# A vision-transformer tower: attention 1's projection and the gates in 16-bit halves, GpSimd adding exponentials and making low halves, and another order of the steps

## The reference

```python
h = layernorm(layernorm(patches) @ W + b)          # 196 x 768 -> 196 x 192, class row put before
x = layernorm(h)
q, k, v = split(x @ w_qkv.T)                        # 12 heads of 64
q, k = q * rsqrt(norm_over_heads(q) + eps), k * rsqrt(norm_over_heads(k) + eps)
h = h + softmax(q k^T / scale) v @ w_out.T + b_out  # attention 1, projection 768 -> 192
x = layernorm(h)
probs = softmax(x @ Wg.T + bg)                      # 8 experts, top 2 kept
delta = low_rank(x, A, ba, Bm, bb, combine)         # rank 16 for each expert
qkv = x @ Wqkv.T + bqkv + delta                     # attention 2, 12 heads of 16
h = h + softmax(q k^T * 0.25) v @ Wproj.T + bproj
```

## Time and profile before

| | |
|---|---|
| median of 3 runs | 3112.13 us (3110.72 to 3112.16) |
| the profiled execution's own time | 3109.35 us |
| its span | 3107.6 us |
| mean granted TensorE clock | 0.988 |
| busy shares of the span | PE 95%, PEld 78%, DVE 75%, ACT 63%, POOL 19% |

### The profile page before, as it was taken

How to read it: one execution, slowest core, us unless ns; L and a number is a source line. 1 busy time by engine, 2 the same in 40 slices (tenths; PEclk the granted TensorE clock), 3 DMA queues, 4 the chain that set the end, 5 groups by cost and what they waited for, 6 DMA issues and landing times.

```text
span 3107.6 us, 98361 instructions
## 1 busy us (share of the span) xinstructions
PE 2962.8 (95%) x41624; PEld 2428.5 (78%) x41624; DVE 2329.0 (75%) x5441; ACT 1963.4 (63%) x3777; POOL 594.1 (19%) x859
## 2 busy tenths in 40 slices
PE   5899999999999999999999999999999999999996
PEld 4788878877877877877877877888788778778775
DVE  5777777777777777777777777777777777777773
ACT  2566666666666666666666666666666666666663
POOL 3112112111111121121121121121121111111210
PEclk7999999999999999999999999999999999999998
DMA  4000000000000000000000000000000000000000
GB/s 116 9 22 22 12 22 16 17 22 12 21 22 12 21 22 12 22 22 12 22 22 12 22 22 12 22 22 12 22 15 18 22 12 21 22 12 22 14 4 7
DMA packets 28389, 61.28 MB, mean 20 GB/s; under 512 B 4210, under 2 KB 18389, under 8 KB 27958
## 3 DMA queue, kind: packets, MB, share of 16 engines
q1 hardware_dynamic: 27958, 54.98, 6.1%
HBM read 45.29 MB, written 9.68 MB: 18 GB/s over the span
## 4 chain that ended last, share of the span: by engine, by line
PE 59%; DVE 35%; ACT 3%; issue 3%; POOL 0%; DMA 0%; SPq 0%; DVEq 0%; ACTq 0%
PE psum L686 9%; DVE mx L1119 8%; PE psum L695 8%; PE psum L590 8%; PE psum L612 7%; PE psum L674 4%; PE psum L722 4%; PE psum L622 4%; DVE st L1008 3%; PE psum L656 3%; DVE mx L1132 2%; PE psum L725 2%; DVE qk L1211 2%; PE psum L732 2%; PE psum L617 2%
## 5 line engine op out<-in xcount | busy, mean ns | idle before, releaser
L850 ACT ACTIVATE ebufs<-psum 99x788 f32<-99x788 f32 x768 | 592.0, 823 | 57.9 <-PE psum L674 45.2
L519 POOL TENSOR_TENSOR veps<-mv,eps_ln 99x2 f32<-99x2 f32 x256 | 116.7, 456 | 2266.5 <-DVE mv L1041 1344.9
L1132 DVE TENSOR_REDUCE mx<-psum 99x4 f32<-99x788 f32 x384 | 357.5, 974 | 137.5 <-PE psum L639 137.2
L1119 DVE TENSOR_REDUCE mx<-psum 99x4 f32<-99x788 f32 x384 | 362.9, 974 | 52.1 <-PE psum L631 52.1
L612 PE MATMUL psum<-hn_s,qk_w 128*128 128x197 f16 x3840 | 354.1, 249 | 14.9 <-DVE hn_s L1083 7.4
L612 PEld LDWEIGHTS psum<-hn_s,qk_w 128*128 128x128 f16 x3840 | 322.2, 97 | 35.6 <-DVE qk L1211 19.0
L686 PE MATMUL psum<-ebufs,vx 98*32 98x197 f32 (+1 forms) x6144 | 293.7, 330 | 0.0
L590 PE MATMUL psum<-emb_w,xb 128*99 128x193 f32 x1536 | 264.0, 327 | 0.0
L695 PE MATMUL psum<-out_w,qk 128*99 128x192 f32 x1536 | 263.8, 328 | 0.1
L590 PEld LDWEIGHTS psum<-emb_w,xb 128*99 128x99 f32 x1536 | 249.1, 166 | 1.4 <-issue 0.9
L686 PEld LDWEIGHTS psum<-ebufs,vx 98*32 98x32 f32 (+1 forms) x6144 | 201.4, 110 | 57.2
(11 more groups left out here) (172 smaller groups left out, 6442.7 us busy)
## 6 DMA issues: line engine op xcount, KB each, us to landing
xb<-x_t SPq DMA_DIRECT2D x64, 591.0 KB, 3.8
out<-h SPq DMA_DIRECT2D x128, 73.5 KB
out<-h SPq DMA_DIRECT2D x64, 0.8 KB
vx<-w_qk SPq DMA_DIRECT2D x2, 384.0 KB, 7.8
qk_sq<-w_emb SPq DMA_DIRECT2D x1, 576.0 KB
vx<-w_qk SPq DMA_DIRECT2D x1, 576.0 KB, 5.6
out_w<-w_out SPq DMA_DIRECT2D x8, 72.0 KB
late<-w_lora_b SPq DMA_DIRECT2D x1, 480.0 KB
```

Source lines behind the costliest of these rows:

```text
L850: nc.scalar.activation(ebuf[n].rearrange("p e a t -> p e (a t)"), psum[0:TR, b + 2 * half:b + 2 * half + 2, 0:2 * NT], ACT.Exp).then_inc(r ...
L1119: nc.vector.tensor_reduce(mx[s][:, :, 2 * i:2 * i + 2].rearrange("p a e -> p e a"), psum[0:TR, b:b + 2, 0:2 * NT].rearrange("p e (a t) -> ...
L1132: nc.vector.tensor_reduce(mx2[s][:, :, at:at + 2].rearrange("p a e -> p e a"), psum[0:TR, b + 2 * half:b + 2 * half + 2, 0:2 * NT].rearran ...
```

## The change

1. **Projection of attention 1 (`OP`).** `out_w` is held in two fp16 halves (split at the start, scaled by 64), and the attention output in `o_h` and `o_l`. ACT copies `o_t` to `o_h` (a new instruction of step `M`), POOL subtracts for `o_l` (a new step `ML.0` to `ML.2`), and PE runs three fp16 matmuls in place of one fp32 matmul: 36 for an image. `OP` waits for `o_low` of `ML.2`.
2. **Gates (`G`).** The weights are split too, and PE takes the fp16 halves of the hidden rows that exist already: 10 fp16 matmuls in place of 4 fp32. ACT's fp32 copy in `T2` is gone.
3. **Sums of exponentials (`PV`).** POOL adds the two key tiles of each `ST` step into `esum` (three buffers), and PE sums 4 matmuls for each `PV` instead of 8; they now stand between the two halves of the product with v. So that the 98-row tile may be added to the 99-row one, row 99 of tile 0 is driven to zero through `head_sel0` and a constant of -30000.
4. **Maxima (`NT`, `NT2`).** The tables `neg` are fp16, and the transposes are fp16 matmuls with an fp16 identity.
5. **Patches.** One buffer `xb` in place of two; the load of the next image is issued after the `EMB` step has read it.
6. **Order.** Another table `ORDER`.

```diff
-+X T1@4 =QK2.0@1 =QK2.1@0 QK.0@2 =SM2.0@4 QK.1@0 QK.2@2 =SM2.1@4 -ST.3@0 -ST.4@4 -ST.5@2 -PV.1@6 S
+QK.0@0 -NT@7 =G@3 =GB QK.1@4 -ST.0@0 -ST.1@2 -ST.2@6 =T3@4 QK.2@0 S -ST.3@6 =QK2.0@2 =QK2.1@5
...
-        xb = two("xb", [128, KC, NT])
+        xb = sb("xb", [128, KC, NT])
...
+        ESUMS = 3
+        esum = [sb(f"esum{i}", [TR, 2, NT]) for i in range(ESUMS)]
...
+                    elif p[0] == "ML":
+                        i = p[2]
+                        wait(pool, now, o_high, ("M", s, i))
+                        nc.gpsimd.tensor_tensor(o_l[s][:, 2 * i:2 * i + 2, :], o_t[s][:, 2 * i:2 * i + 2, :],
+                                                o_h[s][:, 2 * i:2 * i + 2, :], ALU.subtract).then_inc(o_low[1], 1)
+                    elif p[0] == "ST":
+                        wait(pool, now, rd_sig["ST"], p)
+                        n = st_order.index(p) % ESUMS
+                        wait_free(pool, now, esum_users[n], sums_used)
+                        e = exp_tile(p)
+                        nc.gpsimd.tensor_tensor(esum[n][:], e[:, :, 0, :], e[:, :, 1, :], ALU.add
+                                                ).then_inc(tiles_added[1], 1)
...
-                        mm = transposes(p, lambda t, n: table[0:n, t], 128)
+                        for t in range(2):
+                            n = key_rows(t)
+                            mm = nc.tensor.matmul(ps(p, slice(0, 128), slice(TO * t, TO * t + n)),
+                                                  table[0:n, t], ident_h[0:n, 0:n], start=True, stop=True)
...
-                        for c in (2, 0, 1):
+                        for c in (0, 2, 1):
+                            if c == 2:
+                                wait(pe, now, tiles_added, ("ST", s, 2 * i + 1))
+                                for j in range(4):
+                                    es = esum[st_order.index(("ST", s, 2 * i + j // 2)) % ESUMS]
+                                    mm = nc.tensor.matmul(ps(p, slice(32 * j, 32 * j + 32), slice(0, NT), 1),
+                                                          ones_col[:], es[:, j % 2, :], start=True, stop=True)
+                                mm.then_inc(sums_made[1], 1)
+                                continue
...
-                        wait(pe, now, rd_sig["PV"], ("M", s, 2))
+                        wait(pe, now, o_low, ("ML", s, 2))
                         for t in range(2):
                             for m in range(H // 2):
-                                mm = nc.tensor.matmul(ps(p, slice(0, TR), slice(D * t, D * t + D)),
-                                                      o_t[s][:, m, tile_cols(t)], out_w[:, m, :],
-                                                      start=(m == 0), stop=(m == H // 2 - 1))
+                                for n, (left, w) in enumerate(((o_h, 0), (o_h, 1), (o_l, 0))):
+                                    mm = nc.tensor.matmul(ps(p, slice(0, TR), slice(D * t, D * t + D)),
+                                                          left[s][:, m, tile_cols(t)], out_w[:, w, m, :],
+                                                          start=(m + n == 0), stop=(m == H // 2 - 1 and n == 2))
...
-                            for c in range(2):
+                            for n, (w, v, c) in enumerate(PACKED):
                                 mm = nc.tensor.matmul(ps(p, slice(0, TR), slice(136 * t, 136 * t + 136)),
-                                                      hn2_t[s][:, c, tile_cols(t)], gl_w[:, c, :],
-                                                      start=(c == 0), stop=(c == 1))
+                                                      hn2_s[s][:, v, c, tile_cols(t)], gl_w[:, w, :],
+                                                      start=(n == 0), stop=(n == 4))
...
-                        if kind == "T2":
-                            nc.scalar.copy(hn2_t[s], src)
...
+                    elif kind == "M":
+                        wait(act, now, rd_sig["PV"], p)
+                        nc.scalar.copy(o_h[s][:, 2 * i:2 * i + 2, :], o_t[s][:, 2 * i:2 * i + 2, :]).then_inc(o_high[1], 1)
```

More of the change, by code:

```diff
@@ L51 @@
 ORDER = """
-+X T1@4 =QK2.0@1 =QK2.1@0 QK.0@2 =SM2.0@4 QK.1@0 QK.2@2 =SM2.1@4 -ST.3@0 -ST.4@4 -ST.5@2 -PV.1@6 S
--M.1 =SM2.2@0 -PV.2@4 PS@1 =NT2@7 -M.2 N.0 N.1 N.2 +EMB@2 -OP@3 N.3 =ST2.0@4 V.0@0 SM.0@2 =ST2.1@4
--LD =V2@0 SM.1@4 SM.2@2 -T2@6 =PV2.0@7 SM.3@4 =M2.0 =ST2.2@0 =PV2.1@6 SM.4@4 SM.5@0 -G@7 =PV2.2@2
-NT@4 V.1@0 ST.0@4 =M2.1 ST.1@6 +LA =M2.2 -GB +LB ST.2@2 =OP2@5 -T3@4 +LC PV.0@6 M.0
+QK.0@0 -NT@7 =G@3 =GB QK.1@4 -ST.0@0 -ST.1@2 -ST.2@6 =T3@4 QK.2@0 S -ST.3@6 =QK2.0@2 =QK2.1@5
+-PV.0@6 -M.0 -ML.0 =SM2.0@0 PS@4 =V2@6 N.0 -ST.4@0 -PV.1@4 -ST.5@6 -M.1 =SM2.1@0 -ML.1 +X =SM2.2@4
+N.1 -PV.2@0 -M.2 -ML.2 N.2 +EMB@5 =NT2@0 +LA N.3 =ST2.0@0 -OP@6 SM.0@2 SM.1@0 =ST2.1@4 -LD =PV2.0@4
+SM.2@6 =ST2.2@0 =M2.0 =PV2.1@5 +LB V.0@6 =M2.1 -T2@2 =PV2.2@4 +LC SM.3@6 =M2.2 V.1@0 +T1@5 SM.4@2
+SM.5@6 =OP2@4
 """
@@ L243, in vit_tower @@
         o_t = [qk[s][:, 0:H // 2, :] for s in range(2)]
+        o_h = [qk[s][:, 6:9, :].rearrange("p m t -> p (m t)").bitcast(F16).rearrange("p (m t) -> p m t", m=6) for s in range(2)]
+        o_l = [qk[s][:, 9:12, :].rearrange("p m t -> p (m t)").bitcast(F16).rearrange("p (m t) -> p m t", m=6) for s in range(2)]
         gl = two("gl", [TR, 2, NE + NE * RANK])
@@ L353, in reader, with release @@
             return rd_sig[p[0]], ({"PV": "M", "PV2": "M2"}.get(p[0], p[0]), *p[1:])
+        def release(q, freed, earlier):
+            sig, r = freed
+            assert earlier or POS[r] >= POS[q]
+            return sig, r, earlier and POS[r] >= POS[q]
         def wait_free(eng, now, order, freed):
             q, earlier = now.previous(order, now.at)
-            wait(eng, now, *freed(q), earlier)
+            wait(eng, now, *release(q, freed(q), earlier))
         def passes(eng, body):
@@ L401, in vit_tower, with sums_used @@
             bias_loads.append((low_row[r], mats[low:low + NE + 1, 259:261]))
+        st_order = steps["made_ST"]
+        esum_users = [st_order[n::ESUMS] for n in range(ESUMS)]
+        def sums_used(p):
+            return sums_made, ("PV", p[1], p[2] // 2)
         def squares_used(p):
@@ L434, in body @@
                 for kind, s, i in now.steps():
-                    if kind == "QK" and i == 0 and now.which in ("first", "middle"):
+                    if kind == "EMB":
                         wait(sp, now, pe_sig["EMB"], ("EMB", s, 0))
-                        wait(sp, now, xsq_ready, ("X", s, 0))
-                        load(now.it + 1, s)
+                        n = now.image((kind, s, i)) + s
+                        if n < ITERS:
+                            load(n, 1 - s)
                     elif kind == "OP2":
@@ L785, in body @@
                                 act.wait_ge(setup_dve, 2)
-                        nc.scalar.activation(xsq_first if first else xsq, xb[s][:], ACT.Square
+                        nc.scalar.activation(xsq_first if first else xsq, xb[:], ACT.Square
                                              ).then_inc(xsq_ready[1], 1)
@@ L797, in body @@
                     elif kind == "QK":
+                        if now.image(p) == 0 and s == 1 and i == 0:
+                            act.wait_ge(setup_dve, 5)
                         wait(act, now, pe_sig[kind], p)
```

82 lines of the change are left out of this document (50 added, 32 removed).

## The result

The changed kernel takes 3117.67 us (median of 16 runs) against 3111.26 us for the kernel before: ratio 1.002, 95% interval 1.0012 to 1.0028. One of the 16 runs, at a granted clock of 0.647, took 4115.51 us and is left out of the ratio; the median of the other 15 is 3117.58 us. The changed kernel is 0.2% slower, where 1.6% faster was forecast. The page of its profiled execution (3118.04 us) has these rows; the last is the chain of work that ended last, by engine.

The account below looks back on a forecast made before the run. PE's queue, busy 95%, was taken as the bound. 62 half passes at 0.82 us less give 51 us off, 1 us on: 3059 us, plus 2.8 for the median, 3062 us. Range 2985 to 3130 us, the forecast's own 3030 to 3095.

Parts of the forecast that it names:

- rival 1: GpSimd and VectorE block each other around X, so L635 and EMB wait 1.0 us per half pass: 3126 us; chance 0.25.
- the collision of X with N.1 and N.2: X's POOL adds and DVE's N.1, N.2 take turns: 5.3 us together, against 2.55 us for X alone.
- ready 1.7 us early: X starts 4.3 us before L635 asks for its result and, running alone, needs 2.55 us, so no wait.
- a reading in which only instructions as small as L519 are held: On POOL, DVE holds up only very small instructions, so X's adds run free: 3062 us.
- 0.82 us less a half pass: PE's half pass falls from 46.94 to 46.12 us: 2.37 us saved, 1.55 us of waits added.
- the edits: On PE, the OP, gates, sums and transposes edits together save 2.37 us of 43.9 us in a half pass.
- the order: The new table makes PE's waits 4.55 us a half pass against 3.0 now: +1.55 us.
- The gates: PE's G step goes from 1.10 to 0.84 us, priced by weight loads: 0.26 us saved; lower bound 0.62 us.
- Outside the steady part: Start and end: about 2 us of conversions, about 1 us of later load, some 2 us saved in the drain; +1 us.
- rival 2: PE's waits are fewer than walked, 3.0 us a half pass: 2966 us, or halfway there 3010 us; chance 0.23.
- rival 4: OP's fp16 matmuls with 99 weight columns cost 112 ns and more, so OP saves nothing: 3118 us; chance 0.05.
- Rival 3: DVE's queue falls behind by 0.5 us per tile-add collision, QK.0 waits for T1: 3155 us at most; chance 0.05.

Follow-up runs that it names:

- experiment 1: Changed kernel with the second of X's three chained GpSimd adds left out, part of the squares missing: 3083.5 us, ratio 0.991 to the kernel before.
- experiment 10: Changed kernel with attention 2's weights converted later, plus VectorE's N.1 subtraction made to wait for X's three GpSimd adds: 3239.41 us, ratio 1.0412 to the kernel before.
- experiment 4: Kernel before, given only the changed kernel's order table without its ML steps, old arithmetic kept: 3253.23 us, ratio 1.0454 to the kernel before.
- Experiment 6: Changed kernel with the one-time VectorE conversion of attention 2's weights moved behind the maxima of image 0: 3109.45 us, ratio 0.9995 to the kernel before.
- experiment 2: Changed kernel with X moved ahead of M.1 in the order, all computation kept: 3176.62 us, ratio 1.021 to the kernel before.
- 9: Changed kernel with attention 2's weights converted later and X's third slice multiplied on TensorE, two GpSimd adds left: 3096.54 us, ratio 0.9956 to the kernel before.
- experiment 7: Changed kernel with X ahead of M.1 and SM.1's four matmuls issued three times over, same values: 3110.35 us, ratio 0.9997 to the kernel before.
- experiment 3: All arithmetic edits in the order of the kernel before, each ML right behind its M: 3386.65 us, ratio 1.0884 to the kernel before.

## Why the prediction was wrong

- **The step that failed is the choice between forecast and rival 1.** The prediction had found the collision of X with N.1 and N.2, placed it, and given it a quarter of the chances, but its sum put the wait at L635 at nothing ("ready 1.7 us early"). It went by "a reading in which only instructions as small as L519 are held", though the earlier trace rows spoke for the other. The runs decide for it: L525 and L526 are held in 63 of 63 half passes, with one add fewer the kernel is 34 us faster (experiment 1), and with VectorE kept away both adds take 0.53 us again (experiment 10). The Trainium skill says so too ("SBUF — State Buffer", section "Who interferes with whom": an instruction of VectorE with two SBUF inputs and one of GpSimd that reads SBUF exclude each other), and the trace agrees, 1.67 us instead of 0.55. The rival's price was 1.0 us late by its walk; measured are 0.5 to 0.55: X starts 4.5 us before L635 is due and not 4.3, and its chain takes 4.97 us (1557.82 to 1562.79) and not 5.3. Its time, 3126 us, lies near the measured 3117.7 in part by luck: it has 30 us too much for the collision and 20 us too little outside the steady part.
- **Without the collision the steady part was right.** 0.82 us less a half pass was forecast; 47.00 - 46.24 = 0.76 us less was measured in experiment 1. That it came out so near was luck in part, for under it lie two errors that nearly cancel: the edits save 2.7 us and not 2.37 (experiment 4), the order costs 2.0 us and not 1.55. The gates were the mis-sized term of the first: 1.10 to 0.59 us, so 0.51 saved and not 0.26. They took the lower bound of the forecast, by columns (59 ns for each record of 136 columns), and not the price of a weight load. The sums gave 1.08 us for 1.03, `OP` 0.95 for 0.90.
- **Outside the steady part +1 us was forecast; it is +21 us** (16.0 at the start, 4.8 behind the last `EMB`). The prediction counted new conversions, and did not walk the new table through the first two images, where the one-time conversion of attention 2's weights (DVE from 73.5 to 84.9 us) now stands ahead of the maxima of image 0 on DVE. Experiment 6 took 8 us back, of which its profiled execution shows 3.4 at the third `EMB`. L635 of image 1 also waits 2.82 us for X: the patches have landed (`EMB` starts on them at 48.55 us), but ACT comes to their squares only at 51.07 us, behind its part of `PS`, and both short adds are held there too. The order alone (experiment 4) already has its third `EMB` at 109.78 us and 154.5 us behind the last one, though its half passes are 2 us longer. For the end the sums over the stretch behind the last `EMB`, in the columns of experiment 2, before and after, show PE busy for as long as before, at a lower granted clock (0.84 instead of 0.89):

```profile
2958.02:3107.60 149.58, 118.50 (x1650) 95.25 (x1648) 81.97 (x198) 71.64 (x141) 11.45 (x16) 0.89 0.02 6
...
2961.61:3116.00 154.39, 117.91 (x1632) 93.28 (x1628) 84.58 (x200) 70.71 (x142) 32.23 (x38) 0.84 0.02 5
```

Which waits make up the rest of the start and the end stays open.
- **In numbers:** 3062 us forecast, +34 for the collision, +20 outside the steady part, is 3116 us; measured were 3117.7.
- **Rivals 2 to 4** did not occur. Of rival 2, waits fewer than walked, the opposite was measured (2.0 us for the order, not 1.55; its halfway figure of 3010 us is 3014 by its own numbers, and nothing rests on it), and `OP`'s records take 86 ns, not rival 4's 112. Rival 3, a DVE queue that falls behind, is 0 in the changed kernel, but there was little between it and this: in experiment 2 DVE's read of `OP` comes 0.45 us later behind `OP`, and the gap ahead of `ST2.1` is 0.46 us longer.

## What to carry to other kernels

When work moves to GpSimd, list for each of its instructions what VectorE runs at that moment: where both had two operands in SBUF here, the short one ended with the long one (1.67 us against DVE's 1.39), and whatever stands behind it in GpSimd's queue is late as well. To take an instruction away from the collision (experiments 1 and 9) helped, to move it (2) or to hold the other engine (10) did not. Count gaps of TensorE not only by their length: two of 0.9 us close together cost 1.5 us more in clock in 44 of 61 half passes of experiment 2. And walk a new order through the first passes too, since one-time work stands in the same queues.

## What the runs showed of the hardware that was not expected

- TensorE's granted clock fell to its lower level (1.2 GHz) in a half pass in which PE was never idle for a full us: gaps of 0.89 and 0.93 us with 0.9 us of matmuls between them (experiment 2), in 44 of 61 half passes; the expectation of experiment 7 had it in every one. With gaps of 0.43 or 0.54 and 0.93 us it fell in 1 and in 3 of 61 (changed kernel, experiment 7). Redundant matmuls in the gap made the kernel 66 us faster. The Trainium skill ("TensorE: Matmul & The Clock Gate", Part 1) says that the clock follows how busy the engine has been recently; the runs agree in so far as matmuls put into the first gap kept it up. The 0.9 us of work between the two gaps did not.
- The exclusion goes both ways: VectorE's operation on 16 columns took 0.80 us instead of 0.17 against a tile add of GpSimd (experiment 3).
- An fp16 matmul with 99 weight columns and 136 moving columns goes at 59 ns in a row of ten.
